# Layer statistics in two full-width passes, two fewer POOL additions, and a shorter look-ahead, in an eight-core scan kernel

## The reference

```python
def _layernorm(x, axis=-1, eps=1e-5):
    m = jnp.mean(x, axis=axis, keepdims=True)
    v = jnp.var(x, axis=axis, keepdims=True)
    return (x - m) / jnp.sqrt(v + eps)

def attn(xn):                                   # _L0_attn_ref, cut
    x_and_res = xn @ in_proj_w.T + in_proj_b    # 1024 -> 2 x 1024
    x_in = silu(x_and_res[..., :1024]); res = x_and_res[..., 1024:]
    ssm = x_in @ x_proj_w.T + x_proj_b          # 1024 -> 16 + 1024 + 1024
    dlt_raw, Bm, Cm = ssm[..., :16], ssm[..., 16:1040], ssm[..., 1040:]
    delta = clip(softplus(dlt_raw @ dt_proj_w.T + dt_proj_b), 1e-05, 0.1)
    A = clip(-exp(A_log), -5.0, -0.01)          # 1024 x 16
    # for each time step, 16 states for each of 1024 channels:
    #   h = clip(h * exp(A * dt) + B * dt * x, -100, 100)
    #   y = sum(h over the 16 states) * C + D * x
    return y * silu(res) @ out_proj_w.T + out_proj_b

# x = (16, 2048, 1024) float32; ffn is a linear map 1024 -> 1024 (complex product)
out = x + attn(_layernorm(x)) + ffn(_layernorm(x))
```

## Time and profile before

| | us |
|---|---|
| median of 3 runs (lowest, highest) | 2269.91 (2269.84, 2332.44) |
| the profiled execution, its time | 2271.58 |
| its span, slowest core (core 2) | 2269.7 |
| spans of all cores | 2248.4 to 2269.7 |

### The profile page before, as it was taken

One profiled execution on the slowest core, in us unless ns is written; L12 is line 12 of the kernel. 1 busy time (PEld: TensorE's weight loads), 2 busy tenths in 40 slices (PEclk: granted clock), 3 DMA queues, 4 the chain that ended last, 5 costly groups with the idle time before them and its releaser, 6 DMA issues.

```text
span 2269.7 us, 22151 instructions; the slowest of 8 cores (2248.4 to 2269.7 us)
## 1 busy us (share of the span) xinstructions
PE 1245.4 (55%) x5104; PEld 512.6 (23%) x5104; DVE 1610.2 (71%) x1600; ACT 1271.0 (56%) x2001; POOL 630.3 (28%) x570
## 2 busy tenths in 40 slices
PE   1222846265545755485729571967186717764454
PEld 1111313021122322131314130323032213221012
DVE  2331044179976998599939994999589958999970
ACT  0004565485556855695569555965586558754521
POOL 0000131316122352316131713171307131613001
PEclk9999966676676867596859685978597758876556
DMA  5671323620021301130114002310231022202001
GB/s 157 190 176 57 112 74 48 61 59 19 1 84 63 96 19 66 64 114 19 42 70 128 22 28 83 113 37 17 95 99 51 10 102 80 70 1 74 0 10 65
DMA packets 106885, 151.94 MB, mean 67 GB/s; under 512 B 53232, under 2 KB 53240, under 8 KB 106760
## 3 DMA queue, kind: packets, MB, share of 16 engines
q1 hardware_dynamic: 97128, 120.10, 17.9%
q0 software_dynamic: 6176, 19.93, 4.3%
q10 hardware_dynamic: 3456, 10.52, 1.5%
HBM read 124.26 MB, written 26.25 MB: 66 GB/s over the span
## 4 chain that ended last, share of the span: by engine, by line
PE 37%; DVE 21%; issue 12%; ACT 12%; DMA 9%; POOL 7%; SPq 1%; DVEq 0%; ACTq 0%; POOLq 0%
DVE h_buf L839 18%; PE pM L686 6%; PE pS L561 6%; PE pM L651 5%; DMA xr_t<-x 5%; PE pO L589 5%; PE pO L651 4%; PE pO L594 4%; POOL out_tm L477 3%; PE pO L686 3%; ACT da L899 3%; POOL wf L405 1%; PE pT L523 1%; ACT xnf L1002 1%; ACT xin L961 1%
## 5 line engine op out<-in xcount | busy, mean ns | idle before, releaser
L839 DVE TENSOR_TENSOR_SCAN h_buf<-da,cr,Bu 128x512 f16<-128x512 f16 x768 | 1057.0, 1434 | 169.0 <-PE pS L561 164.3
L899 ACT ACTIVATE da<-dlt,ac 128x512 f16<-128x512 f16 x1024 | 694.3, 715 | 330.1 <-DVE h_buf L839 329.0
L561 PE MATMUL pS<-h_buf,eye 128*128 128x512 f16 x1024 | 421.5, 476 | 327.4 <-DVE h_buf L839 314.7
L839 DVE TENSOR_TENSOR_SCAN h_buf<-da,Bu 128x512 f16<-128x512 f16 x256 | 334.5, 1363 | 178.9 <-ACT da L899 122.6
L458 POOL TENSOR_TENSOR Bu<-y_s,sres 128x512 f16<-128x512 f32 x64 | 121.9, 1904 | 786.1 <-DVE y_s L818 786.1
L561 PEld LDWEIGHTS pS<-h_buf,eye 128*128 128x128 f16 x1024 | 108.3, 107 | 563.2 <-issue 501.4
L686 PE MATMUL pM<-xin,rx 128*128 128x512 f16 (+1 forms) x832 | 196.8, 381 | 22.1 <-ACT sres L1034 17.9
L651 PE MATMUL pM<-xnf,rin 128*128 128x512 f16 x512 | 136.8, 417 | 6.6 <-ACT sres L1034 5.2
L477 POOL TENSOR_TENSOR out_tm<-otm,xr_t 128x1024 f32<-128x1024 f16 x32 | 77.8, 2432 | 214.3 <-ACT otm L940 107.9
L589 PE MATMUL pO<-Bu,wo 128*128 128x512 f16 x512 | 134.0, 409 | 3.1 <-POOL Bu L458 3.1
L651 PE MATMUL pO<-xnf,rin 128*128 128x512 f16 x512 | 122.4, 384 | 4.9 <-DMA rin<-wt_in 4.9
(11 more groups left out here) (89 smaller groups left out, 1581.1 us busy)
## 6 DMA issues: line engine op xcount, KB each, us to landing
rin<-wt_in SPq DMA_DIRECT2D x128, 256.0 KB, 2.7
rx<-wt_x SPq DMA_DIRECT2D x128, 256.0 KB, 2.7
x_t<-x SPq DMA_DIRECT2D x32, 512.0 KB, 4.6
xr_t<-x POOLq DMA_DIRECT2D x32, 512.0 KB, 5.0
y<-out_tm SPq DMA_DIRECT2D x32, 512.0 KB, 3.6
wt_in<-rin SPq DMA_DIRECT2D x16, 256.0 KB, 2.4
wt_x<-rin SPq DMA_DIRECT2D x16, 224.0 KB, 3.3
x_t<-w_in ACTq DMA_DIRECT2D x4, 512.0 KB, 3.3
```

What stands on the lines that cost most here:

```text
L561: TCH(te.matmul(sbank[:, :], eye16[:, :], h_sl(gn), start=(n == 0), stop=(n == NST - 1)))
L839: s_n = VCH(v.tensor_tensor_scan(h_sl(gn), da_r[gn % DAR][:, :], Bu[P][k][:, :], init, op0=ALU.mult, op1=ALU.add))
L899: ACH(sc.activation(da_r[gn % DAR][:, :], dlt[Ps][k][:, :], AF.Exp, scale=c_(a_cols[k], n)))
```

## The change

Four edits. (1) ACT's statistics are two passes of 1024 columns instead of four of 512: one Identity with the sum, one Square with the sum of squares. Their unused output goes to `rx[cP % 4]`, the ring place that chunk cP's group 16 will be loaded into, instead of `xin[P][2]`. (2) SP waits for the statistics of the chunk's last tile before it issues the load of group 16. (3) POOL's two additions L433 and L435 and their waits go; the divisions read the sums themselves. (4) The constant in ACT's pump is 10.0 instead of 11.0, in both forms.

```diff
--- before.py
+++ after.py
@@ -347,6 +347,8 @@
                         for _s in range(4):
                             sy.wait_ge(DS["wdt" + str(_s)],
                                        16 * wdt_cnt[_s])
+                    if gi == 16:
+                        wt(sy, "a", ("stats", cP * 4 + 3))
                     if cP >= 1:
                         off = 12 if cP >= 2 else 0
                         if gi < 16:
@@ -430,15 +432,9 @@
                         t = idx
                         g = cP * NTT + t
                         wt(gp, "a", ("stats", g))
-                        s1 = GCH(gp.tensor_add(c_(mcol, t), c_(mcol, t),
-                                               c_(sumx, t)))
-                        s2 = GCH(gp.tensor_add(c_(vcol, t), c_(vcol, t),
-                                               c_(sumsq, t)))
-                        gp.wait_ge(GCH.sem, s1)
-                        s3 = GCH(gp.tensor_scalar(c_(mcol, t), c_(mcol, t),
+                        s3 = GCH(gp.tensor_scalar(c_(mcol, t), c_(sumx, t),
                                                   1.0 / D, None, op0=ALU.mult))
-                        gp.wait_ge(GCH.sem, s2)
-                        GCH(gp.tensor_scalar(c_(vcol, t), c_(vcol, t),
+                        GCH(gp.tensor_scalar(c_(vcol, t), c_(sumsq, t),
                                              1.0 / D, None, op0=ALU.mult))
                         gp.wait_ge(GCH.sem, s3)
                         s4 = GCH(gp.tensor_mul(c_(nmr, t), c_(mcol, t),
@@ -903,9 +899,9 @@
                 def apump(block=False, skip=False):
                     B = bnd[ak[0]]
                     if block:
-                        B2 = bnd[min(ak[0] + 3, len(bnd) - 1)] + 11.0
+                        B2 = bnd[min(ak[0] + 3, len(bnd) - 1)] + 10.0
                     else:
-                        B2 = B + 11.0
+                        B2 = B + 10.0
                     ak[0] += 1
                     if skip:
                         return
@@ -948,24 +944,14 @@
                             wt(sc, "v", ("epi2", (cP - 2) * 8 + 2))
                             wt(sc, "g", ("u", (cP - 2) * 8 + 2))
                         sc.wait_ge(DS["ldx" + str(g % 2)], (g // 2 + 1) * 16)
-                        st1 = ACH(sc.activation(xin[P][2][:, :512],
-                                                x_t[g % 2][:, :512],
+                        dmp = rx[cP % 4][:, 0:1024]
+                        st1 = ACH(sc.activation(dmp, x_t[g % 2][:, :],
                                                 AF.Identity,
                                                 accum_out=c_(sumx, t)))
                         sc.wait_ge(ACH.sem, st1)
-                        st2 = ACH(sc.activation(xin[P][2][:, :512],
-                                                x_t[g % 2][:, 512:],
-                                                AF.Identity,
-                                                accum_out=c_(mcol, t)))
-                        sc.wait_ge(ACH.sem, st2)
-                        st3 = ACH(sc.activation(xin[P][2][:, :512],
-                                                x_t[g % 2][:, :512],
-                                                AF.Square,
-                                                accum_out=c_(sumsq, t)))
-                        sc.wait_ge(ACH.sem, st3)
-                        ACH(sc.activation(xin[P][2][:, :512],
-                                          x_t[g % 2][:, 512:], AF.Square,
-                                          accum_out=c_(vcol, t)))
+                        ACH(sc.activation(dmp, x_t[g % 2][:, :],
+                                          AF.Square,
+                                          accum_out=c_(sumsq, t)))
                         mark(("stats", g), ACH)
                         wt(sc, "g", ("lnv", g))
                         l0 = ACH(sc.activation(c_(rstd, t), c_(vcol, t), AF.Ln,
```

## The result

| | us |
|---|---|
| changed kernel, median of 8 runs (lowest, highest) | 2246.16 (2238.59, 2294.47) |
| kernel before, median of 10 runs | 2270.39 |
| ratio of the fast runs | 0.9881, 95% interval 0.9864 to 0.9897 |
| forecast | 2248 (2236 to 2262) |

A forecast was written before the change was run, and what follows sets the result against it. DVE was taken as the backbone, losing 34.2 us a wave to four statistics waits for PE, with ACT's chain behind them. Gains of 15.3 (waves 2 to 7), 4.7 and 2.2 us, 22.2 in all, gave 2248 us, range 2236 to 2262.

The forecast's parts named there:

- the POOL term: Statistics: removed additions gain 0.42 us in tile 0, elsewhere only the tail behind the burst; refuted above 6 us a wave.
- The passes: ACT's statistics: two wide passes take 2.50 us instead of about 3.26, gaining 0.76 us a tile; bounds 0.40 and 1.64.
- Tile 0: First statistics tile of a wave: gains 0.76 us from passes, 0.42 from POOL, 0.62 from a `da` moved behind the passes.
- Tiles 1 and 2: Tile 1 gains 0.37 us, POOL coming late to it; tile 2 gains 0.55, its first operations ending with the same scans.
- Tile 3: Last statistics tile, a burst of five scans: gain 0.15 to 0.5 us, taken 0.4, including one more `da` before it.
- The reading of the scans' ends: POOL in the statistics: a small operation in a burst lasts until the running scan ends, 1.2 us each; 0.2 after it.
- The third block: In-projection: the shorter look-ahead leaves number 70 to this block, losing 0.56 us a wave; bounds 0 and 1.18.
- Wave 0: No scans; ACT's chain leads to the first in-projection: four tiles gain 0.76 and 0.42 us each, 4.7 us.
- Wave 1: Statistics with bursts: tiles gain 0.55, 0.67, 0.45 and 0.49 us, 2.2 in all, moving the whole rest.
- The full price of the additions: Rival: POOL's additions return their mean, 33 us, and the passes 24, giving 2213 us; chance 0.07.
- Little gain: Rival: passes of 1.43 us, POOL's tail unmoved except with DVE idle, 1.18 lost at third block; 2262 us, chance 0.14.
- Starved scans: Rival: shorter look-ahead costs a 1.18 us scan at many steps; 2301 us at 8 waits a wave; chance 0.05.

The follow-up runs named there:

- e7_orderonly_l11: Changed kernel with look-ahead constant 11.0 and, in POOL's order, statistics tile 1 ahead of the fourth residual addition and block 1's product: 2229.73 us, ratio 0.979 to before.
- e4_pool: Changed kernel with four passes of 512 columns again (two with unused sums), POOL still without its two additions: ratio 0.9944 to the kernel before.
- e1_look: Kernel before with only the look-ahead constant changed, 10.0 instead of 11.0: ratio 0.9991 to the kernel before.
- e2_l11: Changed kernel with the look-ahead constant back at 11.0: median 2243.26 us, ratio 0.9853 to the kernel before.
- e3_passes: Changed kernel with two small POOL additions of a zero column put back where the two were: ratio 0.9935 to the kernel before.
- e8_l12: Changed kernel with look-ahead constant 12.0 in both places: ratio 0.9821 to the kernel before.

## Why the prediction was right

- **The bound.** DVE is the backbone and its waits lie in the statistics: the period of a wave fell by 3.6 us, and the four columns of waits and tiles fell by 4.1, with 0.5 given back in the rest. The forecast had 3.1 and 0.56. In wave 4 of the slowest cores the four waits fell by 5.9 (34.2 to 28.3, where about 31 was forecast), just under the 6 that were to refute the POOL term; part of that is the scatter of the wait ahead of tile 0, part tile 3.
- **The passes, 0.76 us a tile.** The two passes with their accumulator reads take 2.38 us (1129.65 to 1132.03), the four took 3.15 (1140.35 to 1143.50): 0.77. Right, and right that they don't count everywhere.
- **Tile 0, 1.80 with the moved `da`.** The means give 1.66, but the column varies by 2 us and more from core to core; the statistics stretch itself, 1.17, is right to 0.01, and 0.62 for the `da` is one ACT instruction.
- **Tiles 1 and 2, 0.37 and 0.55.** Measured 0.29 and 0.59. `e7_orderonly_l11` shows the reason given for tile 1, `e4_pool` that the passes add nothing there.
- **Tile 3, 0.4.** This is the term that was mis-sized: it measured 1.54 in the mean. The reading of the scans' ends was the right tool, but the step "the subtraction is likely the one that waits for that scan" took one operation through the gap at the carry where two fit, and so counted three held operations where there are two. The step before it, an earlier start of only 0.14 us, is what decides it, and it was passed over as small. Wave 5, in which one operation gets through, gains 0.7, near the forecast; the others gain 1.6 to 1.9. The error makes 1.1 us a wave, 7 us of the whole; with it put right the sum would have been 29.
- **The third block, 0.56 lost.** Measured 0.47 in the changed kernel and 0.57 in `e1_look`, by DVE's own waits there. Right. Beside the 0.62 of tile 0 the forecast took the fourth edit for nearly neutral, and tile 3's one more `da` for a part of a small term; `e2_l11` shows that this `da` costs the tile a whole scan, and the edit 6 us.
- **Wave 0, 4.7 us.** From the first pass to the first in-projection matmul it was 34.0 us on all eight cores and is 29.4. The sign that was named for it, a first in-projection matmul 4.7 us earlier, can't be read from the time of that matmul: what lies ahead of the first pass, the same in both kernels, ends at 185.0 to 190.8 us before and at 186.9 to 197.8 after, so that the matmul starts at 221.6 and 221.2 in the mean of the cores. On core 2 before (189.93 to 223.95) and on core 6 after:

```profile
197.77 1.06 ACT L948 ACTIVATE rx<-x_t 128x1024 f16<-128x1024 f32 x1 [6.10 <-DMA x_t<-x]
```

```profile
227.18 4.89 PE L647 MATMUL pM<-xnf,rin 128*128 128x512 f16 x16 [1.37 <-ACT xnf L998]
```

- **Wave 1, 2.2 us.** From the first scan to the scan after DVE's last long wait in the statistics, 41.50 us became 39.64 on every core within 0.02: 1.9. Whether it moves the whole rest of the wave, as forecast, isn't shown: from the first scan to the first of wave 2 the mean went from 301.6 to 298.4, but single cores lie 6 us apart before and 11 after, and `e2_l11`, with 39.81 in the statistics, has 301.9.
- **The full price of the additions** (2213) fell: `e3_passes` puts the two operations back for 12 us, not 33. **Little gain** (2262) fell: a wide pass with its read is 1.23 us and not 1.43, POOL's tail moved in tiles 1 to 3, the third block cost 0.5 and not 1.18, and the ratio's upper end is 2247. **Starved scans** fell: in waves 2 to 7 DVE waits for ACT at the third block alone. In the rows that wait stands as one for PE (1.27 us, at 1196.64), but the scan there is number 70, and the third block's first `da` starts at 1195.75 on ACT and takes 0.7: to 1196.5. The forecast had "1 us or more"; on the slowest core it is 0.5 to 1.3. **The costs put at nothing** hold: in the whole changed kernel ACT waits for an `x_t` load ahead of a pass once, 6.1 us in wave 0, as before (6.2).
- The forecast that ACT's waits for POOL stay at 13 us missed by the same step: 11.2, tile 3's part being 2.85 instead of 4.65.

The measured parts add up: 6 x 3.6 + 4.6 + 1.9 = 28.1 us, against 27.0 by the ratio, whose interval is 23 to 31. What stays open, beside the rest of wave 1, is the wait ahead of tile 0, which scatters by 2 to 3 us between cores: that the moved `da` is worth 0.62 there is read from ACT's row, and `e1_look`'s 0.36 neither confirms nor refutes it.

## What to carry to other kernels

Where one engine is the backbone, look for the stretch in which it waits, and price a change only there, tile by tile: the same 0.76 us were worth all of it in wave 0, nothing in tile 1, and 1.3 us in tile 3, once POOL had two operations fewer. Small operations of POOL beside a running row of scans cost a scan each, so their number and the moment at which they start count, and a gap of 0.2 us can decide; a look-ahead that moves one instruction across such a gap is worth more than its length. And the larger find was in the wait that the change didn't touch: a load that is issued just before its use, in a chain between two stages, cost some 64 us, more than twice what all the edits brought.

## What the runs showed of the hardware

- A POOL operation on one number a partition takes 0.2 us when DVE is idle or in a carry operation (128 x 4, 0.17 us); in a row of scans it is held until the running scan is over, 1.06 to 1.24 us. What was not expected is that the first scan behind a carry operation still lets one through that starts 0.03 us after it (1164.32 against 1164.29; 40 of 40 in tile 3 of the changed kernel), but not one that starts 0.13 after it (wave 5, 8 of 8); between two scans in a row one that starts as the second does is held for all of it (1166.90). The Trainium skill, SBUF — State Buffer, on the shared port pair, says that whichever starts first holds the pair for its whole length. The trace fits that in the held cases; the operation that passes 0.03 us late goes beyond what it says.
- What is held goes in whole scans: one `da` of 0.62 us fewer ahead of tile 3 made the tile 1.18 us shorter, and in `e8_l12` one fewer again made it no shorter (11.00 in both, and a scan longer in wave 6).
- Reading the accumulator takes ACT 0.19 us, after 512 columns as after 1024. Square and Identity cost the same: the Square's 13 ns more (1056 against 1043) go with its place, as in the kernel before the second Identity takes 629 ns like both Squares, and the first, which doesn't follow an accumulator read, 616.
